# Splitting the MLP weights on GpSimd with one instruction over 2048 columns instead of four over 512

## The chip, the cores and the metric

One Trainium2 chip, one core. The time is device microseconds of one launch; lower is better. The engines of the core are TensorE (matrix products), VectorE, ScalarE, GpSimd and SyncE, which issues the transfers. They run their own instruction streams and wait for each other with semaphores.

## The reference

Two decoder layers on tokens of shape (2, 1024, 256), fp32. The part around the change is layer 0's cross attention MLP and its mixture of 8 experts:

```python
hidden = jax.nn.gelu(out @ W1 + b1, approximate=False)      # cross attention, 256 -> 1024
return hidden @ W2 + b2                                      # 1024 -> 256
...
logits = (xt @ Wr + br) / TEMP
gates = entmax_bisect(logits)                                # 25 bisection steps
gates = jnp.where(gates > THRESH, gates, 0.0)
h = jax.nn.relu(jnp.einsum('td,edf->etf', xt, W1) + b1[:, None, :])   # 8 experts, 256 -> 1024
y = jnp.einsum('etf,efd->etd', h, W2) + b2[:, None, :]                # 1024 -> 256
out = jnp.einsum('etd,te->td', y, gates)
```

Each of these nine MLPs has W1 of 256x1024 and W2 of 1024x256. Before it stands a 16-head self attention over 1024 tokens, after it layer 1 (self attention, cross attention over 64 context tokens, a quantized feed forward). Layer norm follows each block.

## The kernel before

Every fp32 product is made of three passes in the type fp32r: each operand is split into a high part (a copy rounded to fp32r) and a low part (original minus high), and `mm3` (line 87) adds high x high, low x high and high x low.

The MLP stage runs over a sequence of steps n. A job is one expert and one group of 512 tokens (36 jobs, the first four being the cross attention MLP, ex = -1); each job has 8 steps f of 128 hidden units. In step n TensorE makes the first product of step n (6 matmuls 128x512, L1048) and then the second product of step n - LAG, LAG = 2 (12 matmuls 128x256, L1064). All matmuls have line 85 in the profile. For the second product it waits for semaphore m_gl (L1056). Between the two, ScalarE writes the activation twice, as high part m_gh (L1138) and as m_g (L1141), and VectorE makes the low part m_gl = m_g - m_gh (L1279), all three in SBUF, four buffers each. When a job is through, VectorE adds its four tiles from PSUM to X (L1266, L1271).

Between the m_gl, VectorE works through small steps written out as generators: layer norm (`norm_scales`, L237 to L271, on 128x4 tiles, then L318 on X) and gates (`gate_steps`, L1173 to L1241, on 128x8 and 128x64 tiles), up to 10 in one step n. Their place is set by `plan`, a table from n to work: norms after each of the first jobs, the turns of tokens (L1080, L1150, L1302), logits, gates, gated bias (L1315), all through PSUM bank 7.

The weights come by SyncE (`load`, L1384) into raw1 (W1, 128x2x1024) and raw2 (W2, 128x8x256), one MLP after the other. GpSimd (`split`, L1345) makes the high and low parts into one of two sets W of buffers. Split 0 and 1 run ahead, with 16 additions of a bias row to X (L1368) between them; split k for k >= 2 waits until the expert that last used the buffers has ended (m_y at last_of[k-3]), which is `plan`'s "weights". So each split runs beside the products of another expert. TensorE waits for it at the first step of a job (`m_w2`, L1039).

Of the kernel before, what the change touches and what calls it, by code (L numbers as in the profile page):

```python
# [5 lines left out]
F32 = mybir.dt.float32  # L6
# [4 lines left out]
ALU = mybir.AluOpType  # L11
# [11 lines left out]
SEMAPHORES = ("f_va f_rt normed io0 io1 io2 io3 t_xl a_max t_tr a_wp a_pj a_low a_cp a_mhd a_nz a_n a_rw a_exp a_z a_pv "  # L23
              "a_add a_dn a_y a_wo a_ve a_yd c_kT c_qe c_vd ident a_vw a_vp a_zero row0 row1 a_s t_xh a_qk a_wr rows c_kv "
              "a_vr cols c_l1 c_l0 c_l2 c_wqs c_q c_s c_sub c_exp c_E c_e0 c_et c_aT c_o c_oh c_ol m_fin m_w2 m_g0 m_a "
              "m_gl m_y m_gate m_p7 m_gh m_h7 m_gT c_xb m_b7 m_w1 m_r1 m_r2 s_wrl s_w s_z1 s_wpl s_g0 s_g1 s_g2 s_g3 s_n "
              "s_exp s_i s_st s_b7 s_za s_pv s_red x_lk x_lv x_pl s_zm s_p7 s_ip x_qh s_hi s_zd0 s_zd1 s_mhd f_l0 f_l1 "
              "f_iv f_qv x_ql s_nr s_xb x_lq x_lh x_K0 x_K1 x_lm f_qp x_fp x_ev x_z x_lo x_zT x_o x_n x_t x_ex x_s x_q "
              "f_dv f_sp f_xe f_xt x_ft x_mx f_cl f_e4 x_res f_max x_rcp f_dm f_xq f_h f_gu f_hq f_y f_yp f_xa f_xr f_s1 "
# [44 lines left out]
def program(nc, A, out):  # L74
    ctx = ExitStack()
    with ctx:
        s = {n: ctx.enter_context(nc.semaphore(n)) for n in SEMAPHORES}

        def sb(c, name, shape, dt=F32):
            return c.enter_context(nc.sbuf_tensor(name, shape, dt))  # L80
# [41 lines left out]
        with ExitStack() as c1:  # L122
# [14 lines left out]
        raw1, raw2 = sb(cm, "m_raw1", [128, 2, 1024]), sb(cm, "m_raw2", [128, 8, D])  # L137
        Ws = [dict(w1h=sb(cm, f"m_w1h{i}", [128, 2, 1024], FR), w1l=sb(cm, f"m_w1l{i}", [128, 2, 1024], FR),
                   w2h=sb(cm, f"m_w2h{i}", [128, 8, D], FR), w2l=sb(cm, f"m_w2l{i}", [128, 8, D], FR))
# [17 lines left out]
        m_gh = [sb(c, f"m_gh{i}", [128, 512], FR) for i in range(R_M)]  # L157
        m_gl = [sb(c, f"m_gl{i}", [128, 512], FR) for i in range(R_M)]
# [687 lines left out]
        for g in range(4):  # L846
            for turn in range(2):
                n = 8 * (32 * turn + g) + 7 + LAG
# [7 lines left out]
        for g in range(4):  # L856
            n = 50 + 30 * (g // 2) + 4 * (g % 2)
# [470 lines left out]
        def pool_rest(e):  # L1328
            e.wait_ge(s["c_l0"], 16)
            e.tensor_copy(c_wqh[:, :, :], c_wq[:, :, :]).then_inc(s["c_wqs"], 1)  # L1330
            e.wait_ge(s["c_wqs"], 1)
            e.tensor_tensor(c_wql[:, :, :], c_wq[:, :, :], c_wqh[:, :, :].bitcast(F32), ALU.subtract).then_inc(s["c_wqs"], 1)
            e.wait_ge(s["c_l2"], 32)
            e.tensor_copy(m_wrh[:, :, :], m_wr[:, :, :]).then_inc(s["c_wqs"], 1)
            e.wait_ge(s["c_wqs"], 3)
            e.tensor_tensor(m_wrl[:, :, :], m_wr[:, :, :], m_wrh[:, :, :].bitcast(F32), ALU.subtract).then_inc(s["c_wqs"], 1)
            for b in range(B):
                e.memset(c_E[:, 8 * b:8 * b + 8, 64 * (1 - b):64 * (2 - b)], 0.0).then_inc(s["c_e0"], 1)

            def fourth(x, p):  # L1340
                n = x.shape[1]
                return x[:, p // 2, (p % 2) * 512:(p % 2) * 512 + 512] if n == 2 else x[:, 2 * p:2 * p + 2, :]


            def split(k):  # L1345
                W = Ws[k % 2]
                if k >= 2:
                    e.wait_ge(s["m_y"], last_of[k - 3])
                elif k:
                    e.wait_ge(s["a_y"], 16)  # L1350
                else:
                    e.wait_ge(s["a_dn"], 32)
                for r, n, raw in ((1, 4, raw1), (2, 4, raw2)):
                    hi, lo, done = W[f"w{r}h"], W[f"w{r}l"], s["m_w1"] if r == 1 else s["m_w2"]
                    e.wait_ge(s["m_r1"] if r == 1 else s["m_r2"], 16 * (k + 1))
                    for p in range(n):
                        t = e.tensor_copy(fourth(hi, p), fourth(raw, p))  # L1357
                    t.then_inc(done, 1)
                    e.wait_ge(done, 2 * k + 1)
                    for p in range(n):  # L1360
                        t = e.tensor_tensor(fourth(lo, p), fourth(raw, p), fourth(hi, p).bitcast(F32), ALU.subtract)
                    t.then_inc(done, 1)

            split(0)
            e.wait_ge(s["rows"], 16)
            for j in range(NT):
                e.wait_ge(s["t_xl"], 8 + j // 2 + 1)
                e.tensor_tensor(X[:, j, :], X[:, j, :], rows[:, 1, :], ALU.add).then_inc(s["c_xb"], 1)  # L1368
            split(1)
            for n in sorted(plan):  # L1370
                for what in plan[n]:
                    if what[0] == "weights":
                        split(what[1] + 3)
                    elif what[0] == "prepare":
                        e.wait_ge(s["m_y"], last_of[-1])
                        for i, (hi, lo) in enumerate(((s_vh, s_vl), (s_wh, s_wl))):
                            e.wait_ge(s["s_wrl"], 16 * (i + 1))
                            e.tensor_copy(hi[:, :], s_wr[:, :]).then_inc(s["s_w"], 1)
                            e.wait_ge(s["s_w"], 2 * i + 1)
                            e.tensor_tensor(lo[:, :], s_wr[:, :], hi[:, :].bitcast(F32), ALU.subtract).then_inc(s["s_w"], 1)  # L1380
                        e.memset(V1[:, :, :, 16:32], 1.0).then_inc(s["s_z1"], 1)
# [64 lines left out]
        for u in range(N_R + 1):  # L1446
            n = [("natural", 4 * u + i) for i in range(4)] if 2 * u < N_K else []
# [1097 lines left out]
        @block.gpsimd  # L2545
        def _(e):
            pool_l0(e)
            pool_rest(e)
            pool_l1a(e)
            pool_l1x(e)  # L2550
            pool_l1f(e)
# [77 lines left out]
```

## Time and profile before

| | |
|---|---|
| median of 3 runs | 2533.55 us (2524.35 to 2534.45) |
| profiled execution, its own time | 2533.55 us |
| span of its instructions | 2531.8 us |
| TensorE busy | 2381.4 us, 94% |
| VectorE, ScalarE, GpSimd busy | 1566.9, 1314.9, 896.7 us |
| mean granted TensorE clock | 0.974 |

Busy times of different engines overlap. A granted clock of 1.00 is 2.4 GHz and 0.50 is 1.2 GHz. A row of the timeline gives the start in the span, the time taken, engine, line, operation, the tiles written and read, their shapes, how many instructions are merged, and in brackets the idle time of the engine before it and who ended it. A time taken holds the time in which an instruction was already started but held up.

### The profile page before, as it was taken

How to read it: one execution, taken by the hardware profiler on the slowest of the kernel's cores; microseconds unless marked ns; L12 is line 12 of the kernel's file. 1: busy time of each engine (PE TensorE's matmuls, PEld its weight loads, DVE VectorE, ACT ScalarE, POOL GpSimd, SP SyncE). 2: the span in 40 equal slices, each digit the busy share in tenths (PEclk: the TensorE clock that was granted, in tenths of full speed). 3: DMA queues.
4: the chain of work that ended last, by engine and by line, in shares of the span. 5: the costliest groups of instructions: out<-in, count | busy, mean ns of one | idle time of the engine just before them, and what ended most of it. 6: DMA issues, size and time to landing. Idle time of an engine off the chain costs nothing.

```text
span 2531.8 us, 35649 instructions
## 1 busy us (share of the span) xinstructions
PE 2381.4 (94%) x13556; PEld 1709.4 (68%) x13556; DVE 1566.9 (62%) x2919; ACT 1314.9 (52%) x2255; POOL 896.7 (35%) x583
## 2 busy tenths in 40 slices
PE   8999998999999999899999999999799999997775
PEld 7555555855555588888899999999556566654542
DVE  5666663666666355876333333326688878887778
ACT  4566564256655344344444444444166656556766
POOL 3777777077777750201302211301140000031223
PEclk9999999999999999899999999999799999999887
DMA  2001001000100210100101101000333433320001
GB/s 81 13 13 26 13 13 46 13 13 13 26 13 9 81 61 1 34 1 3 65 1 34 34 2 42 9 1 1 94 78 83 97 81 85 93 59 21 1 1 34
DMA packets 55515, 88.12 MB, mean 35 GB/s; under 512 B 11944, under 2 KB 35888, under 8 KB 55344
## 3 DMA queue, kind: packets, MB, share of 16 engines
q1 hardware_dynamic: 55072, 85.70, 12.9%
q8 instruction: 108, 1.77, 0.3%
q14 instruction: 63, 0.52, 0.1%
q10 hardware_dynamic: 272, 0.13, 0.0%
HBM read 37.16 MB, written 2.10 MB: 16 GB/s over the span
## 4 chain that ended last, share of the span: by engine, by line
PE 81%; DVE 8%; ACT 6%; issue 2%; POOL 1%; DMA 1%; SPq 1%; ACTq 0%; DVEq 0%; POOLq 0%
PE PS L85 80%; DVE s_nm L1747 2%; ACT a_P L608 2%; ACT a_QS L557 1%; POOL a_sum L780 1%; ACT x_E L2154 1%; DVE x_sm L2232 0%; DVE s_T L1724 0%; DVE f_am L2419 0%; DVE s_Zd L1770 0%; PE PS L1080 0%; DVE st_s L237 0%; ACT f_Hq L2360 0%; DVE x_rd L2207 0%; PE PS L2045 0%
## 5 line engine op out<-in xcount | busy, mean ns | idle before, releaser
L780 POOL TENSOR_TENSOR a_sum<-a_sum,a_P 128x1024 f32<-128x1024 f32 x192 | 456.0, 2375 | 69.0 <-ACT a_P L608 45.2
L1279 DVE TENSOR_TENSOR m_gl<-m_g,m_gh 128x512 fp32r<-128x512 f32 x288 | 211.4, 734 | 421.6 <-ACT m_g L1141 421.5
L608 ACT ACTIVATE a_P<-PS 128x512 f32<-128x512 f32 x512 | 293.5, 599 | 278.4 <-PE PS L85 270.5
L1138 ACT ACTIVATE m_gh<-PS,cols 128x512 fp32r<-128x512 f32 x288 | 198.5, 689 | 446.0 <-PE PS L85 445.9
L655 DVE TENSOR_REDUCE a_nm<-PS 128x1 f32<-128x1024 f32 x256 | 301.5, 1216 | 130.0 <-PE PS L85 128.3
L1747 DVE TENSOR_REDUCE s_nm<-PS 128x1 f32<-128x512 f32 x512 | 330.9, 682 | 76.6 <-PE PS L85 74.0
L85 PE MATMUL PS<-m_w2h,m_gh 128*128 128x256 f32 x1152 | 323.9, 281 | 3.8 <-DVE m_gl L1279 3.6
L85 PE MATMUL PS<-m_w2l,m_gh 128*128 128x256 f32 x1152 | 323.5, 281 | 0.0
L85 PE MATMUL PS<-m_w2h,m_gl 128*128 128x256 f32 x1152 | 323.3, 281 | 0.0
L1645 ACT ACTIVATE s_P<-PS 128x1024 f32<-128x1024 f32 x256 | 248.2, 1022 | 107.7 <-PE PS L85 107.3
L85 PE MATMUL PS<-a_P,a_V 128*64 128x512 f32 x1024 | 235.5, 602 | 5.0 <-ACT a_Z L581 5.0
L85 PE MATMUL PS<-xh,m_w1h 128*128 128x512 f32 x576 | 232.4, 403 | 0.0
L85 PE MATMUL PS<-a_QS,a_KH 128*128 128x512 f32 x512 | 221.9, 433 | 11.1 <-ACT a_P L608 9.2
L85 PEld LDWEIGHTS PS<-m_w2h,m_gh 128*128 128x128 f32 x1152 | 218.5, 190 | 16.5 <-DVE m_gl L1279 4.4
L85 PE MATMUL PS<-xh,m_w1l 128*128 128x512 f32 x576 | 227.2, 394 | 0.0
L85 PE MATMUL PS<-xl,m_w1h 128*128 128x512 f32 x576 | 226.6, 393 | 0.0
L85 PEld LDWEIGHTS PS<-m_w2h,m_gl 128*128 128x128 f32 x1152 | 219.1, 190 | 11.0
L1357 POOL CAST m_w1h<-m_raw 128x512 fp32r<-128x512 f32 x36 | 23.5, 692 | 557.6 <-PE PS L85 556.3
L85 PEld LDWEIGHTS PS<-m_w2l,m_gh 128*128 128x128 f32 x1152 | 218.5, 190 | 0.0
L85 PE MATMUL PS<-s_K,s_Q 128*128 128x512 f32 x512 | 201.1, 447 | 18.0 <-DVE s_nm L1747 9.0
L85 PE MATMUL PS<-a_QM,a_KL 128*128 128x512 f32 x512 | 201.8, 394 | 2.9 <-DMA a_QM<-a_mh 2.9
L1141 ACT ACTIVATE m_g<-PS,cols 128x512 f32<-128x512 f32 x288 | 196.4, 682 | 0.0
(311 smaller groups left out, 4183.7 us busy)
## 6 DMA issues: line engine op xcount, KB each, us to landing
m_raw<-in_m_w SPq DMA_DIRECT2D x16, 1024.0 KB, 5.3
s_Q<-s_T SPq DMA_DIRECT2D x128, 128.0 KB, 2.4
s_K<-s_T SPq DMA_DIRECT2D x128, 128.0 KB, 2.4
a_KH<-a_KH SPq DMA_DIRECT2D x64, 128.0 KB, 2.4
a_wr<-in_w_qk SPq DMA_DIRECT2D x16, 256.0 KB, 2.9
X<-in_x SPq DMA_DIRECT2D x4, 512.0 KB, 5.9
a_P<-in_w_v SPq DMA_DIRECT2D x8, 256.0 KB, 5.7
m_raw<-in_c_w SPq DMA_DIRECT2D x2, 1024.0 KB, 9.9
```

Source lines behind the costliest of these rows:

```text
L85: return e.matmul(o, l, r, start=start, stop=stop, skip_group_check=shared)
L557: ins = e.activation(QS[i][a][R[a], cs], PS[R[a], bk, :], ACT.Copy, scale=0.125)
L608: e.activation(a_P[:, g % N_P, half * 512:half * 512 + 512], PS[:, s0 + half, :], ACT.Exp).then_inc(s["a_exp"], 1)
L655: e.tensor_reduce(a_nm[:, n % 2, 8 * a + i:8 * a + i + 1], PS[:, bk:bk + 2, :], AX.XY, ALU.max, negate=True).then_inc(s["a_max"], 1)
L780: e.tensor_tensor(o[:, :], a_P[:, (g - 1) % N_P, :] if k == 1 else o[:, :], a_P[:, g % N_P, :], ALU.add).then_inc(s["a_add"], 1)
L1138: e.activation(m_gh[r][:, :], PS[:, 4 + n % 3, :], func, bias=cols[:, bcol:bcol + 1]).then_inc(s["m_gh"], 1)
L1141: e.activation(m_g0[r][:, :], PS[:, 4 + n % 3, :], func, bias=cols[:, bcol:bcol + 1]).then_inc(s["m_g0"], 1)
L1279: e.tensor_tensor(m_gl[r][:, :], m_g0[r][:, :], m_gh[r][:, :].bitcast(F32), ALU.subtract).then_inc(s["m_gl"], 1)
L1357: t = e.tensor_copy(fourth(hi, p), fourth(raw, p))
L1645: e.activation(s_P[w % 4][:, :].rearrange("p (a n) -> p a n", a=2), PS[:, bk:bk + 2, :], ACT.Exp, scale=0.25).then_inc(s["s_exp"], 1)
L1747: e.tensor_reduce(nm2[:, n % 2, i, half:half + 1], PS[:, bank["natural", z], :], AX.X, ALU.max, negate=True).then_inc(s["s_nr"], 1)
L2154: t = e.activation(x_E[j % NE][:, h * 64:h * 64 + 64], PS[:, 2 * (j % 2) + k, (h % 8) * 64:(h % 8) * 64 + 64], ACT.Exp, bias=x_sm[:, j % 3 ...
```

## The change

In `split`, the helper `fourth`, which cut each tile into four pieces of 512 columns, is gone. Each of the four operations of a split (high part of W1, low part of W1, high part of W2, low part of W2) is now one instruction over 128x2048 in place of four over 128x512. The semaphore waits and increments are the same: each group had one increment, on its last piece. In the list of semaphores m_r1 and m_w1 change places.

```diff
--- before.py
+++ after.py
@@ -23,7 +23,7 @@
 SEMAPHORES = ("f_va f_rt normed io0 io1 io2 io3 t_xl a_max t_tr a_wp a_pj a_low a_cp a_mhd a_nz a_n a_rw a_exp a_z a_pv "
               "a_add a_dn a_y a_wo a_ve a_yd c_kT c_qe c_vd ident a_vw a_vp a_zero row0 row1 a_s t_xh a_qk a_wr rows c_kv "
               "a_vr cols c_l1 c_l0 c_l2 c_wqs c_q c_s c_sub c_exp c_E c_e0 c_et c_aT c_o c_oh c_ol m_fin m_w2 m_g0 m_a "
-              "m_gl m_y m_gate m_p7 m_gh m_h7 m_gT c_xb m_b7 m_w1 m_r1 m_r2 s_wrl s_w s_z1 s_wpl s_g0 s_g1 s_g2 s_g3 s_n "
+              "m_gl m_y m_gate m_p7 m_gh m_h7 m_gT c_xb m_b7 m_r1 m_w1 m_r2 s_wrl s_w s_z1 s_wpl s_g0 s_g1 s_g2 s_g3 s_n "
               "s_exp s_i s_st s_b7 s_za s_pv s_red x_lk x_lv x_pl s_zm s_p7 s_ip x_qh s_hi s_zd0 s_zd1 s_mhd f_l0 f_l1 "
               "f_iv f_qv x_ql s_nr s_xb x_lq x_lh x_K0 x_K1 x_lm f_qp x_fp x_ev x_z x_lo x_zT x_o x_n x_t x_ex x_s x_q "
               "f_dv f_sp f_xe f_xt x_ft x_mx f_cl f_e4 x_res f_max x_rcp f_dm f_xq f_h f_gu f_hq f_y f_yp f_xa f_xr f_s1 "
@@ -1337,11 +1337,6 @@
             for b in range(B):
                 e.memset(c_E[:, 8 * b:8 * b + 8, 64 * (1 - b):64 * (2 - b)], 0.0).then_inc(s["c_e0"], 1)
 
-            def fourth(x, p):
-                n = x.shape[1]
-                return x[:, p // 2, (p % 2) * 512:(p % 2) * 512 + 512] if n == 2 else x[:, 2 * p:2 * p + 2, :]
-
-
             def split(k):
                 W = Ws[k % 2]
                 if k >= 2:
@@ -1350,16 +1345,16 @@
                     e.wait_ge(s["a_y"], 16)
                 else:
                     e.wait_ge(s["a_dn"], 32)
-                for r, n, raw in ((1, 4, raw1), (2, 4, raw2)):
-                    hi, lo, done = W[f"w{r}h"], W[f"w{r}l"], s["m_w1"] if r == 1 else s["m_w2"]
-                    e.wait_ge(s["m_r1"] if r == 1 else s["m_r2"], 16 * (k + 1))
-                    for p in range(n):
-                        t = e.tensor_copy(fourth(hi, p), fourth(raw, p))
-                    t.then_inc(done, 1)
-                    e.wait_ge(done, 2 * k + 1)
-                    for p in range(n):
-                        t = e.tensor_tensor(fourth(lo, p), fourth(raw, p), fourth(hi, p).bitcast(F32), ALU.subtract)
-                    t.then_inc(done, 1)
+                e.wait_ge(s["m_r1"], 16 * (k + 1))
+                e.tensor_copy(W["w1h"][:, :, :], raw1[:, :, :]).then_inc(s["m_w1"], 1)
+                e.wait_ge(s["m_w1"], 2 * k + 1)
+                e.tensor_tensor(W["w1l"][:, :, :], raw1[:, :, :], W["w1h"][:, :, :].bitcast(F32),
+                                ALU.subtract).then_inc(s["m_w1"], 1)
+                e.wait_ge(s["m_r2"], 16 * (k + 1))
+                e.tensor_copy(W["w2h"][:, :, :], raw2[:, :, :]).then_inc(s["m_w2"], 1)
+                e.wait_ge(s["m_w2"], 2 * k + 1)
+                e.tensor_tensor(W["w2l"][:, :, :], raw2[:, :, :], W["w2h"][:, :, :].bitcast(F32),
+                                ALU.subtract).then_inc(s["m_w2"], 1)
 
             split(0)
             e.wait_ge(s["rows"], 16)
```

## Rows read from the trace of the kernel before

**Rows 1.** The page's first part: busy time, share and instructions of each engine.

```profile
PE 2381.4 (94%) x13556; PEld 1709.4 (68%) x13556; DVE 1566.9 (62%) x2919; ACT 1314.9 (52%) x2255; POOL 896.7 (35%) x583
```

**Rows 2.** Busy time per stretch: start:end, length, engines (instructions), PEclk, DMA.

```profile
1420.00:1500.00 80.00, 80.00 (x519) 72.97 (x518) 28.14 (x45) 36.15 (x58) 17.12 (x16) 1.00 0.08 27
...
1036.83:1056.40 19.57, 13.11 (x72) 11.03 (x71) 19.09 (x53) 5.06 (x8) 15.99 (x16) 0.91 0.27 86
```

**Rows 3.** Timelines, VectorE beside GpSimd: start us, us, engine, line.

```profile
909.40 0.17 DVE L246 TENSOR_SCALAR st_r<-st_a 128x4 f32<-128x4 f32 x1
...
1051.76 1.25 DVE L254 TENSOR_SCALAR st_r<-st_r 128x4 int32<-128x4 int32 x1
...
2341.12 1.90 POOL L2270 TENSOR_TENSOR x_E<-x_E,x_rd 128x1024 f32<-128x1024 f32 x1 [5.84 <-DVE x_rd L2214]
...
2341.24 1.80 DVE L246 TENSOR_SCALAR st_r<-st_a 128x4 f32<-128x4 f32 x1
```

**Rows 4.** Timeline of a steady split, from 1242 us: GpSimd, VectorE, TensorE.

```profile
1242.32 2.70 POOL L1357 CAST m_w1h<-m_raw 128x512 fp32r<-128x512 f32 x4 [33.03 <-PE PS L85]
...
1242.79 1.65 DVE L1271 SCALAR_TENSOR_TENSOR X<-PS,m_G,X 128x256 f32<-128x256 f32 x4
1244.96 0.69 DVE L1279 TENSOR_TENSOR m_gl<-m_g,m_gh 128x512 fp32r<-128x512 f32 x1 [0.52 <-ACT m_g L1141]
...
1250.52 1.04 DVE L1279 TENSOR_TENSOR m_gl<-m_g,m_gh 128x512 fp32r<-128x512 f32 x1 [1.91 <-ACT m_g L1141]
...
1249.02 0.28 PE L85 MATMUL PS<-m_w2h,m_gh 128*128 128x256 f32 x1
```

**Rows 5.** GpSimd lines: ns min/median/max, first and last start.

```profile
L1334 POOL CAST m_wrh<-m_wr x1: 196/196/196, 873.5 to 873.5; 128x16 fp32r<-128x16 f32 x1
L1330 POOL CAST c_wqh<-c_wq x1: 610/610/610, 871.5 to 871.5; 128x512 fp32r<-128x512 f32 x1
L1332 POOL TENSOR_TENSOR c_wql<-c_wq,c_wqh x1: 1268/1268/1268, 872.2 to 872.2; 128x512 fp32r<-128x512 f32 x1
L780 POOL TENSOR_TENSOR a_sum<-a_sum,a_P x192: 2340/2378/2408, 62.6 to 862.0; 128x1024 f32<-128x1024 f32 x192
L1381 POOL MEMSET s_V<- x1: 1812/1812/1812, 1622.7 to 1622.7; 128x2048 f32 x1
```

**Rows 6.** The split at 1037 us: TensorE's waits, and GpSimd and VectorE.

```profile
PE PS L85 <- DVE m_gl L1279: 3.6, 2, 2.7
PE PS L1080 <- DVE X L318: 2.9, 1, 2.9
...
1047.44 5.55 POOL L1361 TENSOR_TENSOR m_w2l<-m_raw,m_w2h 128x512 fp32r<-128x512 f32 x4
...
1045.17 1.16 DVE L1279 TENSOR_TENSOR m_gl<-m_g,m_gh 128x512 fp32r<-128x512 f32 x1
...
1054.72 0.68 DVE L1279 TENSOR_TENSOR m_gl<-m_g,m_gh 128x512 fp32r<-128x512 f32 x1
...
1055.54 0.73 DVE L318 TENSOR_SCALAR X<-X,st_a,st_r 128x256 f32<-128x256 f32 x2
...
1058.10 0.68 DVE L1279 TENSOR_TENSOR m_gl<-m_g,m_gh 128x512 fp32r<-128x512 f32 x1
```

**Rows 7.** VectorE's m_gl during the splits at 923 and at 1192 us.

```profile
931.34 0.69 DVE L1279 TENSOR_TENSOR m_gl<-m_g,m_gh 128x512 fp32r<-128x512 f32 x1 [4.83 <-ACT m_g L1141]
...
1206.36 1.78 DVE L1279 TENSOR_TENSOR m_gl<-m_g,m_gh 128x512 fp32r<-128x512 f32 x1 [2.40 <-ACT m_g L1141]
```

**Rows 8.** Two waits of TensorE (us, times, longest) and the windows after them.

```profile
PE PS L85 <- DVE s_nm L1747: 2.0, 2, 1.6
...
PE PS L892 <- DVE xl L904: 1.6, 1, 1.6
...
861.00:868.00 7.00, 5.38 (x31) 3.26 (x30) 4.49 (x6) 3.33 (x6) 3.25 (x2) 1.00 0.34 101
...
2224.60:2227.90 3.30, 3.30 (x20) 1.68 (x20) 2.95 (x8) 0.65 (x2) 3.08 (x4) 0.50 0.01 2
```

## The prediction

> **What bounds the kernel now.** I read the page's first part first: TensorE is busy 2381.4 of 2531.8 us, VectorE 1566.9, GpSimd 896.7 [rows 1]. So a time is moved only by what makes TensorE wait. The edit touches the nine places where GpSimd splits a set of MLP weights, between 876 and 1615 us. The windows of that stage show two kinds of stretch [rows 2]: from 1180 us on TensorE is busy in 80.00 of every 80 us, while GpSimd works 17 and VectorE 28 us in it; in the 19.57 us of the split at 1037 us TensorE is busy 13.11 only and VectorE 19.09. The first kind has no wait at all to take away; the second hangs on VectorE. GpSimd's own speed binds nowhere: split k writes the weights of a later expert. In the steady part a step takes 2.78 us (two m_gl, 1244.96 and 1250.52, are two steps apart [rows 4]), an expert has 32, so a split comes every 89 us and has all of these for its 17.
>
> **Why GpSimd's instruction length matters.** On VectorE an L246 on 128x4 took 0.17 us at 909.40 with GpSimd idle, and 1.80 us at 2341.24, started 0.12 us after a GpSimd instruction of 1.90 us (2341.12) and ended with it; an L254 on 128x4 took 1.25 us beside pieces of a split's subtract of 1.27 us [rows 3, 5]. So a VectorE operation of this kind (two inputs in SBUF, or tensor_scalar on SBUF) waits for the whole running GpSimd instruction, then goes, then GpSimd goes again: with both waiting they alternate. GpSimd is held in the same way: the first four casts of the split at 1242 us take 2.70 us, where 4 x 0.61 = 2.44 is the most for free ones. Operations that read PSUM aren't held: the four L1271 that run beside the casts take 1.65 us [rows 4], 0.41 each. The one that is both of the held kind and on TensorE's path is m_gl (L1279: m_g and m_gh, both in SBUF), 0.69 us when free (1244.96 [rows 4]). Now it is held for one piece at most, 1.27 us; after the change for one whole instruction.
>
> The Trainium skill ("SBUF — State Buffer", section "SBUF: two separate sides") says that VectorE and GpSimd share one port pair as an exclusive lock kept for the full instruction. The rows agree up to 1.90 us; nothing before the change is longer with SBUF inputs than 2.4 us. By that rule a 2048-wide instruction holds m_gl over its whole length, which speaks against the change; a lock let go inside a long instruction is rival 2.
>
> **The change part by part.** (a) *Fewer instructions on GpSimd.* 9 x 16 become 9 x 4. The cast: 0.61 us for 512 columns, 0.196 for 16 [rows 5], so (0.610-0.196)/496 = 0.83 ns a column and 0.61+1536 x 0.00083 = 1.89 us for 2048, near the 1.81 us of the memset on 2048 [rows 5]; bounds: that and 4 x 0.61 = 2.44. The subtract: 1.27 us for 512, 2.378 for 1024 [rows 5], 2.16 ns a column, so 1.27+1536 x 0.00216 = 4.59, say 4.55; bounds 4.2 (a little under two of 1024) and 5.08 (4 x 1.27). The split alone falls from 14.6 to about 13 us. That lies beside TensorE's work: worth 0 on the path, except at 1037 us.
>
> (b) *Semaphores in another order, the helper gone.* The same waits with the same counts: 0. The loads of SP wait on m_w1 and m_w2 at 2k as before and come 1 us earlier: 0, as the next split is 70 us away.
>
> (c) *Five steady splits* (k = 4 to 8, at 1242, 1331, ... 1598 us; one stands in [rows 4], the other four repeat it 89 us apart). Step by step: the cast starts at 1242.32 and is held by the m_gl that ends as L1271 begins, till about 1242.75; cast 1.89, to 1244.65; the subtract starts 0.06 later, 1244.7. m_gl is ready at 1244.96, just too late, and is held till 1249.1; ends 1249.75. What TensorE can bear: it multiplies this m_gl at 1249.02 [rows 4], and m_gl ended at 1244.96+0.69 = 1245.65, so the slack is 3.36 us. First wait: 1249.8-1249.02 = 0.8 us. Queued behind on VectorE: the next m_gl, ready at 1244.96+2.78 = 1247.74. The second cast asked first, runs 1249.65 to 1251.55, that m_gl ends at 1252.15: TensorE needs it at 1249.02+2.78+0.8 = 1252.6, no wait. Next the long subtract 1252.0 to 1256.5; the m_gl ready at 1250.52 ends at 1257.15. It would have ended at 1251.21: 5.94 late, less the slack of 3.36 = 2.6 us in all. The next one, 1257.75, is needed at 1249.02+3 x 2.78+2.6 = 1260.0: caught up. ScalarE's reuse of the m_g buffers is bound to the m_gl of four steps ago (11.1 us), so it stays out. 5 x 2.6 = 13 us. If m_gl wins the first race (it comes only 0.26 us after the lock is taken), the same walk gives: subtract 1245.6 to 1250.0, then cast, then subtract 1252.9 to 1257.3, whose m_gl (ready 1253.30) ends 3.95 late: 0.6 us each, 3 in all.
>
> (d) *The split at 1037 us* (k = 2). VectorE interleaves norm and gate steps between the m_gl, nearly all of the held kind; TensorE waited 3.6 us for m_gl and 2.9 for X of L318 [rows 6]. With four long instructions VectorE gets one held operation between each: L1195, L1199, L1207, then L1221 when the last subtract ends. By the lengths of (a), from 1036.83 on, that is at 1036.83+0.5+2 x 1.89+2 x 4.55+0.5 of handing over = 1050.7 (now 1047.44+5.55 = 1052.99). The remaining chain is 0.5 us to the m_gl that started at 1045.17, 3.4 to the next (the free interval between 1054.72 and 1058.10), 3.56 less the stall of L254 (1.25-0.17) = 2.5 to the third, 1.55 to the end of the second L318 [rows 3, 6]: 1050.7+0.5+3.4+2.5+1.55 = 1058.6, against 1056.27 in [rows 6] (1055.54+0.73). +2.4, say 2.5 us; bounds -2 (if long instructions hold nothing more, the split ending 2.2 earlier) and +5.7 (the first m_gl's own delay, if TensorE makes up nothing).
>
> (e) *The other splits.* k = 3 (1192 us): bank 7 work (L1315) stands between its m_gl, so its steps are longer than 2.78 us; one m_gl there took 1.78 us after 2.40 us of idle VectorE, and TensorE didn't wait [rows 7]. By the walk of (c) its m_gl end up to 4.2 late; the slack is 3.36 and a microsecond or more of that work: 0. k = 1 (923 us): VectorE is idle for 4.83 us before an m_gl [rows 7], the steps are up to 5.5 us; delays of up to 4.1 fit: 0. k = 0: L246 and the chain behind it are held for one subtract, at most 4.55 us in place of 4 held operations of 1.2, then alternate with L1368: 0. Bounds for the three together 0 and 3.
>
> (f) *The clock.* After a wait of TensorE of 1.6 us for L1747 (in a total of 2.0) the granted clock was 0.50, which is 1.2 GHz, in 2224.6 to 2227.9; after one of 1.6 us for L904 it stayed at 1.00 [rows 8]. In the steady splits it is 1.00 now. New waits of 0.8 and 1.8 us lie at the edge. A stretch of 3.4 us at half speed costs a bound TensorE 1.7 us. I take half of the five: 5 x 0.5 x 1.7 = 4.2; bounds 0 and 8.5.
>
> Sum: 13+2.5+0+4.2 = 19.7, say 20 us. The profiled execution took 2533.55, the same as the median of the three, so 2533.5+20 = 2553.5.
>
> The Trainium skill ("GPSIMD Engine Reference", section "3.1 Elementwise — side-by-side cycle accounting") gives 4.497 us for a tensor_tensor of 2048 fp32 columns on GpSimd. With 4.50 in place of 4.55 the sum would be 0.5 us lower; no row here has that width yet.
>
> **The rivals.** 1. *m_gl wins the race* at the start of each steady split: 3+2.5+1 for the clock = +6.5, 2540. For: the margin is 0.26 us and the cast's length is extrapolated (at 2.2 us it flips). Against: three rows give 1.81 to 1.89. Chance 0.17. 2. *A long instruction lets the lock go inside* (not slower): VectorE is held no longer than now, and only GpSimd's saved starts remain: 0 in the steady splits, -2 at 1037 us where the split ends sooner: 2531.5. It decides in place (c): it holds when no m_gl there takes over 2 us. Against: 1.80 us held of 1.90; for: nothing longer was seen held. Chance 0.13. 3. *The clock falls at every one of the five waits and the split at 1037 us loses 5.7*: 13+5.7+8.5 = +27, with the subtract at its bound of 5.08 each split loses 3.6 rather than 2.6: +32, 2566. Chance 0.1. My forecast: 0.6.
>
> **How the numbers follow.** My own case spans 2546 (no fall of the clock) to 2562. To hold 8 in 10 I add rival 1 and most of 3: 2536 to 2567; left out are rival 2 and the far ends. A measurement here tells no change from 0.5%, 12.7 us: slower above 2546.2. Slower: nearly all of the forecast (0.56) and rival 3 (0.1), and a little of rival 1: 0.69. Same: rival 1, rival 2 and the rest: 0.27. Faster: 0.04 (the three times of before themselves span 10 us).
>
> **What would show it.** The splits as 18 casts of about 1.9 us and 18 subtracts of about 4.5. In the five steady splits the longest m_gl near 4.8 us, a second one of 3 to 5, two waits of TensorE for L1279 of 0.8 and 1.8, TensorE's waits for L1279 up from 3.6 to 17 or more; L318's wait changed at 1037. No new waits at 923 and 1192. The clock at 0.50 after some of them. Wrong if m_gl stays under 2 us (rival 2), or if the first m_gl of a steady split takes 0.69 (rival 1), or if the alternation fails and GpSimd's instructions run back to back while VectorE waits: then the delays add up and it is far slower.

## The result and the profile after

The changed kernel took 2548.36 us (median of 5, 2544.86 to 2550.21) against 2534.45 for the kernel before (5 runs, 2524.35 to 2540.41). The ratio is 1.0053 with a 95% interval of 1.0037 to 1.0069; 17 executions of the changed kernel are on record, from 2541.65 to 2551.71. It is slower by 13.9 us in the medians, by about half a per cent: the interval holds neither 1 nor a loss above 0.7%. That is inside the forecast range of 2536 to 2567, 5 us under the forecast of 2553.5. The profiled execution took 2551.71 us, its span is 2548.4.

The page's first part, as in [rows 1]. GpSimd is busy for 24 us less, and the span is longer all the same: the time that GpSimd saved bought nothing.

```profile
PE 2387.8 (94%) x13547; PEld 1710.2 (67%) x13556; DVE 1624.9 (64%) x2919; ACT 1314.2 (52%) x2255; POOL 872.9 (34%) x475
```

The timelines of the first steady split, answering to [rows 4]: GpSimd, then VectorE's m_gl, then the two matmuls of TensorE that waited, with the wait in brackets.

```profile
1245.84 2.31 POOL L1349 CAST m_w1h<-m_raw 128x2048 fp32r<-128x2048 f32 x1 [35.57 <-PE PS L85]
1248.23 4.61 POOL L1351 TENSOR_TENSOR m_w1l<-m_raw,m_w1h 128x2048 fp32r<-128x2048 f32 x1
1252.78 2.36 POOL L1354 CAST m_w2h<-m_raw 128x2048 fp32r<-128x2048 f32 x1
1255.22 4.93 POOL L1356 TENSOR_TENSOR m_w2l<-m_raw,m_w2h 128x2048 fp32r<-128x2048 f32 x1
...
1248.48 4.91 DVE L1279 TENSOR_TENSOR m_gl<-m_g,m_gh 128x512 fp32r<-128x512 f32 x1 [0.52 <-ACT m_g L1141]
...
1253.31 2.38 DVE L1279 TENSOR_TENSOR m_gl<-m_g,m_gh 128x512 fp32r<-128x512 f32 x1
...
1255.61 5.09 DVE L1279 TENSOR_TENSOR m_gl<-m_g,m_gh 128x512 fp32r<-128x512 f32 x1
...
1253.44 0.38 PE L85 MATMUL PS<-m_w2h,m_gh 128*128 128x256 f32 x1 [0.74 <-DVE m_gl L1279]
...
1260.75 0.39 PE L85 MATMUL PS<-m_w2h,m_gh 128*128 128x256 f32 x1 [1.42 <-DVE m_gl L1279]
```

The four groups of GpSimd are four instructions now, 2.31 (0.4 of it held by the m_gl before), 4.61, 2.36 and 4.93 us. The m_gl that began at 1248.48, 0.25 us after the subtract, took 4.91 us in place of 0.69 and ended at 1253.39, 0.55 us after the subtract (1252.84). The next one, 1253.31, was held by the second cast and ended 0.55 us after it, and the third, 1255.61, was held by the second subtract and again ended 0.55 us after it. TensorE waited 0.74 and 1.42 us. This is the walk of part (c), event by event: it gave 0.8 and 1.8.

TensorE's waits from 1200 to 1640 us (in total, times, longest), and the first cast of the last steady split, in the changed kernel and in the kernel before:

```profile
PE PS L85 <- DVE m_gl L1279: 10.8, 10, 1.4
```

```profile
1612.72 2.31 POOL L1349 CAST m_w1h<-m_raw 128x2048 fp32r<-128x2048 f32 x1 [77.41 <-PE PS L85]
...
1598.16 2.70 POOL L1357 CAST m_w1h<-m_raw 128x512 fp32r<-128x512 f32 x4 [71.67 <-PE PS L85]
```

Ten waits, two in each of five splits. From the first cast of the first steady split (1245.84) to that of the fifth (1612.72) the changed kernel takes 366.88 us. In the kernel before these are 1242.32 [rows 4] and 1598.16: 355.84 us. The difference is 11.04 us for four splits, 2.76 each, 13.8 for five. The waits in the rows make only 2.16 a split, so each costs TensorE about 0.3 us more than it shows: a wait's row counts from the modelled end of the last matmul, 0.40 us after its start, where the next starts after 0.24 when nothing waits; and behind a wait the second matmul starts 0.22 us after the first, not 0.12. With that the two waits cost about 1.0 and 1.7 us.

The granted clock in the steady part (start:end, length, TensorE, its loads, VectorE, ScalarE, GpSimd, PEclk, DMA):

```profile
1337.00:1360.00 23.00, 20.84 (x133) 18.28 (x132) 16.74 (x12) 9.24 (x15) 14.15 (x4) 1.00 0.28 92
1262.00:1337.00 75.00, 75.00 (x488) 68.42 (x487) 22.72 (x38) 33.77 (x54) 0.00 (x0) 1.00 0.04 13
```

It is 1.00, which is 2.4 GHz, in a window with two of these waits as in one without, and in every stretch of 10 us from 1240 to 1640. None of the ten waits drew the clock down.

The split at 1040 us, answering to [rows 6]: TensorE's waits for m_gl over the whole stage, VectorE's held steps, the matmul that waited, the clock behind it, and TensorE's first matmul on the normed X (L1080).

```profile
PE PS L85 <- DVE m_gl L1279: 18.6, 11, 7.8
...
1042.56 4.53 DVE L1203 TENSOR_TENSOR m_D<-m_L,m_sc 128x64 f32<-128x64 f32 x1
1047.12 1.80 DVE L1207 SCALAR_TENSOR_TENSOR m_D<-m_D 128x64 f32<-128x64 f32 x1
...
1049.21 4.22 DVE L1221 SCALAR_TENSOR_TENSOR m_sc<-m_sc 128x8 f32<-128x8 f32 x1
...
1053.95 0.68 DVE L1279 TENSOR_TENSOR m_gl<-m_g,m_gh 128x512 fp32r<-128x512 f32 x1
...
1054.69 0.58 PE L85 MATMUL PS<-m_w2h,m_gh 128*128 128x256 f32 x1 [7.83 <-DVE m_gl L1279]
...
1050.00:1063.00 13.00, 8.31 (x39) 7.55 (x40) 12.52 (x51) 1.87 (x3) 3.41 (x1) 0.61 0.36 124
...
1061.47 0.60 PE L1080 MATMUL PS<-ident,X 128*128 128x128 f32 x4
```

One wait of 7.8 us for m_gl stands in place of 3.6 for m_gl and 2.9 for L318. Each of L1203, L1207 and L1221 was held by one GpSimd instruction (the first subtract, the second cast, the second subtract), as the alternation demands. The m_gl itself took 0.68: it stood in VectorE's queue behind them. Yet from this split to the next (1040.00 to 1195.93, 155.93 us) little is lost: before it was 1036.83 to 1192.41, 155.58. The clock was at 0.50 from about 1050.0 to 1060.2 (0.61 in the mean of 1050 to 1063), and 4.7 us of that fall into the wait, where they cost nothing.

By stretches, from the first cast of a split to that of another (the first ends at split 0, the last begins with split 8, so one split's loss is in it):

| stretch, us | before | after | difference |
|---|---|---|---|
| start of span to split 0 | 876.14 | 878.92 | +2.8 |
| splits 0 to 2 | 160.69 | 161.08 | +0.4 |
| split 2 to 3 | 155.58 | 155.93 | +0.35 |
| split 3 to 4 | 49.91 | 49.91 | 0 |
| split 4 to 8 | 355.84 | 366.88 | +11.04 |
| split 8 to the end | 933.6 | 935.6 | +2.0 |

The stretch from split 4 to 8 is the one that can be read to a hundredth: in the kernel before and in every kernel below without a wait there it takes 355.84 or 355.85 us. The stretch from split 2 to 3 can't: with the same four pieces it took 155.58, 157.14 (wide late) and 152.35 us (order of the semaphores), one profile each, so +0.35 is no measured cost. The first stretch holds no changed instruction. Its clock differs (0.99 in the mean to 860 us for 1.00 before), and its +2.8 makes the profiled span's 16.6 us more than the 13.9 of the medians.

### The profile page after: what moved, and what is told of

Same layout as the page of the kernel before. It is cut to its first block, busy times and chain, and to the rows that moved or that the text cites. A ratio compares the mean times of both kernels' runs of the same rounds, so it can differ in the third digit from the quotient of the medians.

```text
span 2548.4 us, 35532 instructions
## 1 busy us (share of the span) xinstructions
PE 2387.8 (94%) x13547; PEld 1710.2 (67%) x13556; DVE 1624.9 (64%) x2919; ACT 1314.2 (52%) x2255; POOL 872.9 (34%) x475
## 3 DMA queue, kind: packets, MB, share of 16 engines
q8 instruction: 107, 1.75, 0.3%
## 4 chain that ended last, share of the span: by engine, by line
PE 79%; DVE 10%; ACT 6%; issue 2%; POOL 1%; DMA 1%; SPq 1%; another core or an unknown queue 0%; ACTq 0%; DVEq 0%; POOLq 0%
PE PS L85 78%; DVE m_gl L1279 2%; DVE s_nm L1742 2%; ACT a_P L608 2%; ACT a_QS L557 1%; POOL a_sum L780 1%; ACT x_E L2149 1%; DVE x_sm L2227 0%; DVE s_T L1719 0%; DVE s_Zd L1765 0%; PE PS L1080 0%; DVE f_am L2414 0%; ACT f_Hq L2355 0%; DVE x_rd L2202 0%; ACT m_g L1141 0%
## 5 line engine op out<-in xcount | busy, mean ns | idle before, releaser
L1279 DVE TENSOR_TENSOR m_gl<-m_g,m_gh 128x512 fp32r<-128x512 f32 x288 | 267.1, 933 | 382.6 <-ACT m_g L1141 382.6
L1349 POOL CAST m_w1h<-m_raw 128x2048 fp32r<-128x2048 f32 x9 | 20.0, 2221 | 588.5 <-PE PS L85 587.3
```

The costliest lines, as they stand in the source:

```text
L1279: e.tensor_tensor(m_gl[r][:, :], m_g0[r][:, :], m_gh[r][:, :].bitcast(F32), ALU.subtract).then_inc(s["m_gl"], 1)
L1349: e.tensor_copy(W["w1h"][:, :, :], raw1[:, :, :]).then_inc(s["m_w1"], 1)
```

## The experiments

Each kernel was timed beside the kernel before on the same chip; its medians there were 2532.19 us (beside halves, wide subtracts, wide early and wide late), 2532.18 (order of the semaphores, wide casts, memset, eighths) and 2532.70 (the pads, spread, memsets in split 2). Ratios are to those, with a 95% interval. The edits are shortened to the lines that matter, against the kernel before or the changed one.

**Halves.** Two pieces of 1024 columns for all four operations.

```diff
-    e.tensor_copy(W["w1h"][:, :, :], raw1[:, :, :])
+    for p in range(2):      # columns 1024 p to 1024 p + 1023, the same for the three others
+        t = e.tensor_copy(hi[:, 1024 * p:1024 * p + 1024], raw[:, 1024 * p:1024 * p + 1024])
```

> Two pieces of 1024 columns for each operation of each split. Theory (an m_gl is held for one whole GpSimd instruction, and TensorE bears 3.36 us): a subtract of 1024 takes about 2.36 us, so no m_gl is more than about 2.5 us late in the five steady splits, TensorE has no wait there, and the time is that of the kernel before (within 4 us). Rival (the loss comes from having fewer instructions, or from GpSimd running closer together): about half of the change's 14 us, 2541.

Measured: 2533.57 us, 1.0007 (0.9996 to 1.0017). The m_gl (min/median/max ns) and the first steady subtract, two instructions:

```profile
L1279 DVE TENSOR_TENSOR m_gl<-m_g,m_gh x288: 674/693/2864, 919.1 to 1776.1; 128x512 fp32r<-128x512 f32 x144
...
1247.95 5.21 POOL L1354 TENSOR_TENSOR m_w1l<-m_raw,m_w1h 128x1024 fp32r<-128x1024 f32 x2
```

No m_gl took more than 2.86 us, 2.2 more than a free one, under the 3.36 that TensorE bears; no wait in the steady part, which takes 355.84 us. The theory holds: half as many instructions as before cost nothing.

**Wide subtracts only.** Casts in four pieces, subtracts over 2048 columns.

```diff
-    for p in range(4):
-        t = e.tensor_tensor(fourth(lo, p), fourth(raw, p), fourth(hi, p).bitcast(F32), ALU.subtract)
+    t = e.tensor_tensor(lo, raw, hi.bitcast(F32), ALU.subtract)
```

> Casts in four pieces, subtracts over 2048 columns. Theory of the race: four casts end some 0.4 us later than the wide one, after the m_gl that is ready 2.64 us into the split, so that m_gl takes 0.69 us; the long subtract then meets only the m_gl behind it, which has time: longest m_gl about 2.7 us in the first half of the split, no wait or at most 0.6 us a split, 0 to 3 us in all. Rival (length alone: any hold of 4.5 us costs TensorE about 1 to 2.8 us): the five steady splits lose as in the changed kernel, about 14 us in all.

Measured: 2531.68 us, 0.9998 (0.9989 to 1.0007). First steady split and the first casts of the last:

```profile
1241.35 2.71 POOL L1356 CAST m_w1h<-m_raw 128x512 fp32r<-128x512 f32 x4 [34.68 <-PE PS L85]
1244.14 5.02 POOL L1354 TENSOR_TENSOR m_w1l<-m_raw,m_w1h 128x2048 fp32r<-128x2048 f32 x1
...
1252.41 5.09 POOL L1354 TENSOR_TENSOR m_w2l<-m_raw,m_w2h 128x2048 fp32r<-128x2048 f32 x1
...
1243.99 0.69 DVE L1279 TENSOR_TENSOR m_gl<-m_g,m_gh 128x512 fp32r<-128x512 f32 x1 [0.52 <-ACT m_g L1141]
...
1246.78 2.94 DVE L1279 TENSOR_TENSOR m_gl<-m_g,m_gh 128x512 fp32r<-128x512 f32 x1 [2.09 <-ACT m_g L1141]
...
1597.19 2.71 POOL L1356 CAST m_w1h<-m_raw 128x512 fp32r<-128x512 f32 x4 [72.81 <-PE PS L85]
```

Here the subtract starts at 1244.14, 0.15 us behind the m_gl of 1243.99, is itself held by it (5.02 us in place of 4.6), and the m_gl behind, 1246.78, takes 2.94. From 1241.35 to 1597.19 it is 355.84 us, as before. The instructions that hold for 4.6 us are all there, and cost nothing: it is not their length alone but also when they begin. The rival falls.

**Wide early, wide late.** The same two forms, chosen by the split's number.

```diff
+    pieces = 1 if k < 4 else 4      # wide early; wide late has them the other way round
```

> Wide instructions in splits 0 to 3 only, four pieces in splits 4 to 8. Theory (the time is lost in the steady splits alone): like the kernel before within 4 us; TensorE waits about 7.8 us for m_gl at 1040 us in one piece and no more for L318. Rival (the split at 1040 us with its wait of 7.8 us carries the loss): 2540 or more.

> Four pieces in splits 0 to 3, wide in splits 4 to 8. Theory: the whole loss, 5 x 2.76 = 13.8 us over the kernel before, with waits of 0.74 and 1.42 us in each of the five. Rival (the early splits carry it): within 4 us of the kernel before.

Measured: early 2534.38 us, 1.0001 (0.9990 to 1.0012); late 2547.43, 1.0057 (1.0039 to 1.0074). The loss is in splits 4 to 8, as far as can be told (the early kernel's interval allows 3 us either way), though the largest single wait, 7.9 us for m_gl at 1045 us, is in the early kernel.

**Order of the semaphores.**

```diff
-              ... m_b7 m_w1 m_r1 m_r2 ...
+              ... m_b7 m_r1 m_w1 m_r2 ...
```

> The kernel before with only the places of m_r1 and m_w1 in the list of semaphores changed. Theory: nothing, ratio 1.000 within its interval. Rival: the numbering of the semaphores matters; then a part of the 14 us stands here.

Measured: 2532.88 us, 1.0004 (0.9993 to 1.0015): nothing.

**Wide casts only.**

```diff
-    for p in range(4):
-        t = e.tensor_copy(fourth(hi, p), fourth(raw, p))
+    t = e.tensor_copy(hi, raw)
```

> Casts over 2048 columns, subtracts in four pieces. Theory: a cast holds an m_gl for at most 1.9 us, under the 3.36 us that TensorE bears: no wait in the steady splits, time of the kernel before. Rival (any long instruction costs): some us more.

Measured: 2531.58 us, 0.9990 (0.9981 to 0.9999); no wait in the steady splits, m_gl up to 1.75 us there. As the theory has it.

**A pad before the long subtracts.** On the changed kernel, memsets of a spare 128x128 tile: two before the subtract of W1, and in a second kernel also four before that of W2.

```diff
     e.tensor_copy(W["w1h"][:, :, :], raw1[:, :, :]).then_inc(s["m_w1"], 1)
+    for _ in range(2):
+        e.wait_ge(pads.sem, pads.n)
+        e.memset(m_pad[:, :], 0.0).then_inc(pads.sem, 1)
+        pads.up()
     e.wait_ge(s["m_w1"], 2 * k + 1)
```

> The changed kernel with two memsets of 128x128 on a spare tile, some 0.5 us, between the cast and the subtract of W1 in every split. A memset held no VectorE operation in the run before, so this only lets GpSimd come later. Theory of the race: the m_gl ready 2.64 us into a steady split gets through in 0.69 us, the long subtract ends later and the wait of 0.74 us is gone; the second subtract, which begins just before the m_gl that is ready at 10.98, still holds that one, for about 1 us of waiting: 5 x 1 = 5 us over the kernel before in place of 14, 2537. Rival (length alone): more GpSimd time, the loss stays at 14 us or grows.

Measured: 2539.34 us, 1.0021 (1.0011 to 1.0031). GpSimd, the third m_gl behind the pad, and TensorE's waits in the steady part:

```profile
1246.64 0.47 POOL L1347 MEMSET m_pad<- 128x128 f32 x2
1247.07 5.13 POOL L1362 TENSOR_TENSOR m_w1l<-m_raw,m_w1h 128x2048 fp32r<-128x2048 f32 x1
...
1254.59 4.95 POOL L1368 TENSOR_TENSOR m_w2l<-m_raw,m_w2h 128x2048 fp32r<-128x2048 f32 x1
...
1255.37 4.72 DVE L1280 TENSOR_TENSOR m_gl<-m_g,m_gh 128x512 fp32r<-128x512 f32 x1 [0.31 <-ACT m_g L1142]
...
PE PS L85 <- DVE m_gl L1280: 2.8, 5, 0.6
```

With 0.38 us between cast and subtract in place of 0.08 the first wait is gone. The second subtract still begins at 1254.59, ahead of the m_gl of 1255.37, which takes 4.72 us: five waits, 2.8 us in all. The steady stretch is 359.23 us, 0.85 more a split, 4.2 in all. This is rival 1 of the prediction, brought about by the pad: it put 0.6 a split. The time is 6.6 us over the median of before, 5.3 by the ratio (2.8 to 7.9); what the steady part does not hold of it is not assigned.

> As the run with a pad before the first subtract, and four such memsets, some 1.0 us, before the subtract of W2 as well. Theory of the race: both long subtracts now begin while an m_gl holds them up, the m_gl behind is at most 2.5 us late, no wait is left in the steady splits: the time of the kernel before, within 3 us, with instructions of full length. Rival (length alone): the loss stays at 14 us.

Measured: 2534.39 us, 1.0009 (1.0000 to 1.0018). The pads, the second subtract, and the m_gl that now comes first:

```profile
1254.54 0.99 POOL L1347 MEMSET m_pad<- 128x128 f32 x4
1255.50 5.12 POOL L1368 TENSOR_TENSOR m_w2l<-m_raw,m_w2h 128x2048 fp32r<-128x2048 f32 x1
...
1255.45 0.69 DVE L1280 TENSOR_TENSOR m_gl<-m_g,m_gh 128x512 fp32r<-128x512 f32 x1 [0.31 <-ACT m_g L1142]
```

Now 1255.50 comes 0.05 us behind 1255.45. No wait is left in the steady part, and the stretch is 355.84 us again. So with instructions of this length the 13.8 us come from which engine asks first at each of the two long subtracts. In the changed kernel GpSimd is 0.25 us ahead at the first, and VectorE is behind from then on.

**Memset in place of the subtract.** Leaves out the low parts of the weights.

```diff
-    e.tensor_tensor(W["w1l"][:, :, :], raw1[:, :, :], W["w1h"][:, :, :].bitcast(F32), ALU.subtract)
+    e.memset(W["w1l"][:, :, :].bitcast(F32), 0.0)      # the same for w2l
```

> Leaves out the low parts of the weights: each wide subtract is one memset of 128x2048 in its place, about 1.8 us, which reads nothing in SBUF. If only GpSimd instructions that read SBUF hold a VectorE operation with two SBUF inputs, the m_gl that is ready 2.64 us into a steady split takes 0.69 us though the memset runs. If every GpSimd instruction holds it, it takes about 2.1 us. Either way TensorE does not wait, and the time is that of the kernel before within the run's noise.

Measured: 2521.98 us, one run. The first steady split begins at 1233.40 here; its memset and second cast, and the m_gl beside each:

```profile
1235.77 1.81 POOL L1351 MEMSET m_w1l<- 128x2048 f32 x1
1237.52 1.90 POOL L1353 CAST m_w2h<-m_raw 128x2048 fp32r<-128x2048 f32 x1
...
1236.04 0.69 DVE L1279 TENSOR_TENSOR m_gl<-m_g,m_gh 128x512 fp32r<-128x512 f32 x1 [0.52 <-ACT m_g L1141]
...
1238.82 1.14 DVE L1279 TENSOR_TENSOR m_gl<-m_g,m_gh 128x512 fp32r<-128x512 f32 x1 [2.09 <-ACT m_g L1141]
```

The m_gl that is ready 2.64 us into the split runs inside the memset and takes 0.69 us: the memset does not hold it. The next one, 1238.82, begins 0.60 us before the end of the cast and takes 1.14: the cast does. The expectation on the time fell: it is 10 us under the kernel before, and from split 2 to 3 it takes 147.15 us in place of 155.58. That the holding at 1037 us costs so much wasn't in the prediction, and led to the last two experiments.

**Eighths.** 256 columns a piece.

```diff
-    for p in range(4):      # 512 columns
+    for p in range(8):      # 256 columns
```

> Eight pieces of 256 columns for each operation. Theory: a held VectorE operation waits at most 0.7 us. No gain in the steady splits, which have no wait already. At 1037 us VectorE gets more held operations in per microsecond, so TensorE's waits there (3.6 for m_gl, 2.9 for L318 before) shrink by 1 to 3 us: 2531 to 2534, not to be told from the kernel before by the time. Rival (more instructions cost more): GpSimd's split grows to 19 us or more and the waits at 1037 us grow with it.

Measured: 2530.19 us, 0.9989 (0.9980 to 0.9998). TensorE's waits from 1030 to 1110 us:

```profile
PE PS L1080 <- DVE X L318: 5.2, 1, 5.2
PE PS L85 <- DVE m_gl L1279: 0.6, 1, 0.6
```

The wait for m_gl shrinks from 3.6 to 0.6, the one for L318 grows from 2.9 to 5.2: 6.0 in all with L1271's 0.2, of 6.7. VectorE gets more steps in, and GpSimd's split takes 19.2 us in place of 16.2. The gain of 1 to 3 us in the waits was not reached (0.7), and the waits did not grow with GpSimd's 19 us as the rival has it; what the time gains is at the edge of what can be told.

**Spread.** The 16 pieces of split 2 spread over 12 steps of TensorE.

```diff
+    def spread(k, c):
+        if k == 2 and c:
+            e.wait_ge(s["m_y"], last_of[-1] + 3 * c // 4)
...
     for p in range(n):
+        spread(k, 8 * (r - 1) + p)
         t = e.tensor_copy(fourth(hi, p), fourth(raw, p))
```

> The kernel before with the 16 pieces of split 2 (the one at 1037 us) spread: piece c waits until TensorE is 3c/4 steps further. Theory (GpSimd keeps VectorE from its held operations there without a break, and VectorE has the time to make that up if it comes spread out): TensorE's waits at 1037 us fall from 6.5 us to under 3, and the time by 3 to 8 us against the kernel before, 2525 to 2529. Rival (VectorE is short of time over the whole stretch of gates and norms, so it doesn't matter when it is held): within 1 us.

Measured: 2532.23 us, 0.9992 (0.9980 to 1.0004). TensorE's waits, 1030 to 1110 us:

```profile
PE PS L1080 <- DVE X L318: 3.4, 1, 3.4
PE PS L85 <- DVE X L1271: 1.7, 1, 1.7
PE PS L85 <- DVE m_gl L1279: 0.6, 1, 0.6
```

5.7 us of waits against 6.7. The rival stands: moving the holding within this stretch gives nothing back that can be told.

**Memsets in split 2 only.** Leaves out the low parts of one set of weights, those of expert 1; four pieces everywhere.

```diff
     for p in range(n):
-        t = e.tensor_tensor(fourth(lo, p), fourth(raw, p), fourth(hi, p).bitcast(F32), ALU.subtract)
+        t = e.memset(fourth(lo, p).bitcast(F32), 0.0) if k == 2 else e.tensor_tensor(...)
```

> The kernel before, leaving out the low parts of the weights of split 2 alone: its eight subtract pieces are memsets. It shows what the holding at 1037 us costs the kernel before at most by its subtracts. Theory: TensorE's waits there fall to about 2 us and the time by 5 to 8 us. Rival (the stretch is bound by VectorE's own work): within 1 us.

Measured: 2520.36 us, 0.9953 (0.9940 to 0.9966), 12.3 us under the kernel before, more than the 5 to 8 expected. GpSimd's memsets, VectorE steps beside them, TensorE's wait for L318, and the windows of the stretch to split 3:

```profile
1037.64 1.93 POOL L1362 MEMSET m_w1l<- 128x512 f32 x4
...
1038.61 0.17 DVE L1225 SCALAR_TENSOR_TENSOR m_sc<-m_sc 128x8 f32<-128x8 f32 x1
...
1039.01 0.58 DVE L1195 TENSOR_SCALAR m_sc<-m_sc 128x8 f32<-128x8 f32 x1
...
1041.98 1.97 POOL L1362 MEMSET m_w2l<- 128x512 f32 x4
...
1042.48 0.51 DVE L246 TENSOR_SCALAR st_r<-st_a 128x4 f32<-128x4 f32 x1
...
PE PS L1080 <- DVE X L318: 1.4, 1, 1.4
...
1034.00:1180.00 146.00, 144.38 (x932) 129.52 (x931) 112.97 (x456) 64.56 (x103) 8.95 (x16) 1.00 0.05 15
```

Split 2 to split 3 takes 145.24 us, 10.3 less than before. The waits of TensorE fall from 6.7 to 1.6 us, which is half of it; the other half is the clock, 1.00 in the whole stretch here. In the profile of before, 10.2 us of the stretch were at 1.2 GHz; at half speed these cost 5.1 us of work.

This sum holds in all 14 profiles (before, after, and the experiments): the stretch, less TensorE's waits, less half of the time that TensorE worked at 1.2 GHz, is 143.3 to 143.8 us. The waits repeat, the clock does not: in the three profiles with four pieces in split 2 the waits are 6.7, 6.7 and 6.9 us, and the time at half clock 10.2, 13.7 (wide late) and 3.4 us (order of the semaphores). So of what this experiment gave back, 5.1 us are the waits; the clock's part is 5.1 against the one profile and would be 1.7 against another. And not every fall of the clock follows a wait. In the kernel before, the last of the 24 matmuls of the logits, and the window behind them:

```profile
1066.90 0.25 PE L85 MATMUL PS<-m_wrl,xh 128*128 128x8 f32 x1
...
1068.00:1070.00 2.00, 2.00 (x8) 1.65 (x7) 1.06 (x6) 0.41 (x1) 0.00 (x0) 0.50 0.00 0
```

The last wait before that ended at 1056.41; the same happened at 1030 us, also behind 24 such matmuls, with no wait of TensorE from 950 us on. Two of the three spans of 3.4 us at half clock in the stretch came just behind a wait, the third behind these matmuls. In the kernel of this experiment the same 24 matmuls stand at both places, and the clock stays at 1.00. What draws it down there is not shown.

## Why the prediction was right, point by point

**What bounds the kernel.** Confirmed: GpSimd's busy time fell by 24 us and the kernel got slower by 14.

**The hold lasts as long as the GpSimd instruction, and the two alternate.** The longest m_gl was 5.09 us (0.69 free). In the split shown one m_gl gets in behind each GpSimd instruction. The Trainium skill's rule ("SBUF — State Buffer", section "SBUF: two separate sides") that the lock is kept for the full instruction holds at 4.6 us as it did at 1.9: each held m_gl ended only after the instruction that held it. Rival 2, a lock let go inside a long instruction, fell.

**(a) Lengths.** Cast 1.89 predicted, 1.88 to 1.90 measured where free; subtract 4.55 predicted (its own line gives 4.59), 4.49 to 4.63 measured where little or nothing held it. The Trainium skill's 4.497 us ("GPSIMD Engine Reference", section "3.1 Elementwise — side-by-side cycle accounting") is as close.

**(b) Semaphores.** 0 predicted; 1.0004 measured for them alone.

**(c) Five steady splits.** 2.6 us each predicted, 2.76 measured; 13 and 13.8 in all. The loss is there, and as far as can be told only there (early 1.0001, late 1.0057). The walk let the first subtract end at 1249.1 where its own 1244.7+4.55 gives 1249.25, which changes nothing. The race was forecast with a margin of 0.26 us and was 0.25. That the forecast came out on the right side of so small a margin was in part luck. The experiments with pads show that for instructions of this length the margin decides: rival 1 appears as soon as GpSimd comes 0.3 us later, at 4.2 us in all where 3 were put for it. Halves show that the length matters too: its m_gl are held, for up to 2.86 us, and it loses nothing.

**(d) The split at 1037 us.** +2.5 predicted; +0.35 in the profile, less than profiles of the same code differ by, and nothing measurable in the early kernel (1.0001). The step that failed, a small one, is that the walk took the end of the second L318 as what TensorE waits for. That end did come 1.7 us later after the split's start (21.2 for 19.4; I had 21.8), but TensorE did not wait for it: it came to L1080 at 1061.47, 0.3 us behind it, without a wait, since it had lost its time before, in the one wait of 7.8 us for m_gl. TensorE's waits in the stretch rose from 6.7 to 8.0 us only, and its work at half clock fell from 10.2 to about 9 us, because 4.7 us at half clock fell into the wait. A wait there can't be priced without the clock.

**(e) The other splits.** 0 predicted, 0.4 and 0.0 measured. In the split that begins at 1196 us an m_gl took 4.18 us and TensorE did not wait for it.

**(f) The clock.** 4.2 us predicted, 0 measured. This is the term that was mis-sized, and the largest part of the 5.8 us between the sum of 19.7 and the measured 13.9; (d) adds 2.2 to the gap, and (c) and (e), 0.8 and 0.4 short, take 1.2 of it away. The sum without this term is 15.5 us, 2549 (the prediction says 2546 for that case), 0.6 us from the measured time: closer than its terms are, by errors that offset each other. Waits of 0.74 and 1.42 us, 6 us apart in an otherwise unbroken run of matmuls, left the clock at 2.4 GHz ten times of ten. The row I leaned on [rows 8], a wait of 1.6 us with the clock down behind it, came from the self attention of layer 1, where TensorE waits at many places (3.6 us for L1747 in six waits from 2150 to 2225 us). That this is why it was no match for an isolated wait is not shown.

What stays open: why the profile after shows other states of the clock before 880 us, where nothing was changed, and what draws the clock down from split 2 to 3, with and without a wait in front. The 12.3 us of the last experiment are shown as the gain of taking the subtracts of split 2 out; 5.1 of them are waits. How much of the rest is the clock there is known for single profiles only, and in that profile 2.9 us are gone before split 2 already, where nothing was changed. A version that computes the same and takes this holding away wasn't found. Two kernels, wide casts (0.9990) and eighths (0.9989), come out just under the kernel before, with intervals that end at 0.9999 and 0.9998; the 2 us are less than profiles of the same code differ by, so neither is claimed as better.

## What to carry to other kernels

Before merging GpSimd instructions, look for VectorE operations with two SBUF inputs (or tensor_scalar on SBUF) on the critical path: each can be held for one whole GpSimd instruction. Here pieces well below the slack of the next consumer, 3.36 us, cost nothing (subtracts over 1024 columns), and instructions of 4.6 us cost 13.8 us, 4.2 or nothing, by which engine asked first, with margins of 0.25 us and less. So compare the longest GpSimd instruction with that slack first. Held operations also queue: the third m_gl of a split ended 5.9 us late by the walk, more than one hold. A size that relies on winning such a race can lose it by 0.3 us elsewhere, as the pads show the other way round. GpSimd's saved starts, 0.14 us each (the first split, with nothing beside it, takes 12.98 us in place of 14.66), were worth nothing here, where it is off the path.

## What the hardware showed beyond that

A GpSimd memset does not hold VectorE operations with two SBUF inputs (the m_gl of 0.69 us inside a memset of 1.81), but it does hold tensor_scalar on SBUF: in the rows of the last experiment L1195 and L246 take 0.58 and 0.51 us beside memsets, and 0.17 when free. The recorded expectation that a memset held no VectorE operation was too wide by these. The Trainium skill ("SBUF — State Buffer", section "SBUF: two separate sides") makes the same distinction: an operation with two SBUF inputs is held only by a GpSimd operation that reads SBUF.

A wait of TensorE of 1.42 us between full runs of matmuls left the clock at 2.4 GHz in five cases, and one of 0.74 us in five. In the stretch of gates and norms behind 1037 us the clock was at 1.2 GHz for 3.4 to 13.7 us in three profiles of the same code, with 6.7 to 6.9 us of waits each. The two kernels with memsets in place of the subtracts of split 2 had 0 and 3.4 us of it.
